# Two slots of 16 pairs in place of three, spare products on TensorE, and a first slot in three parts

## The reference

```python
# x, u: 8192 x 64, adj: 8192 x 8192, all float32
keep = (u >= 0.1)
x_drop = x * keep / 0.9
y = x + adj @ x_drop
out = (y - mean(y)) / sqrt(var(y) + 1e-5)      # over the 64 columns of each row
```

## Time and profile before

| | |
|---|---|
| median of 3 runs | 642.97 us |
| the profiled execution's own time | 643.25 us |
| its span, first to last instruction | 641.5 us |
| mean granted TensorE clock | 0.927 of full |
| TensorE busy | 514.2 us (80%) |
| VectorE, ScalarE, GpSimd busy | 48.6, 10.8, 18.0 us |
| DMA: moved, mean rate | 274.80 MB, 428 GB/s |

### The profile page before, as it was taken

How to read it: one execution, slowest core, us unless ns; L and a number is a source line. 1 busy time by engine, 2 the same in 40 slices (tenths; PEclk the granted TensorE clock), 3 DMA queues, 4 the chain that set the end, 5 groups by cost and what they waited for, 6 DMA issues and landing times.

```text
span 641.5 us, 5637 instructions
## 1 busy us (share of the span) xinstructions
PE 514.2 (80%) x2308; PEld 175.9 (27%) x2308; DVE 48.6 (8%) x230; ACT 10.8 (2%) x18; POOL 18.0 (3%) x27
## 2 busy tenths in 40 slices
PE   0397888778988797797788779788797788689796
PEld 0132223222222232232232223222232232223225
DVE  2100101010010100101010010100001010000102
ACT  0000000000000000000000000000000000000000
POOL 0000000000000000000000000000000000000000
PEclk9998888998979798898989989798898989989999
DMA  9999999999999999999999999999999999999998
GB/s 374 423 448 436 429 432 440 416 440 425 430 436 450 412 449 440 429 426 443 413 440 429 430 432 454 426 432 443 423 430 439 420 437 447 428 416 428 434 422 335
DMA packets 9962, 274.80 MB, mean 428 GB/s; under 512 B 1388, under 2 KB 1642, under 8 KB 2666
## 3 DMA queue, kind: packets, MB, share of 16 engines
q1 hardware_dynamic: 9660, 274.60, 99.5%
q10 hardware_dynamic: 300, 0.16, 0.1%
HBM read 272.66 MB, written 2.10 MB: 428 GB/s over the span
## 4 chain that ended last, share of the span: by engine, by line
DMA 70%; PE 27%; issue 1%; SPq 0%; DVE 0%; POOL 0%; POOLq 0%; ACT 0%; DVEq 0%
DMA raw<-adj_dram 70%; PE acc L173 26%; SPq L132 0%; PE turned L193 0%; POOL rstd L268 0%; DVE stats L238 0%; POOLq L47 0%; ACT sums L211 0%; DVE rows L234 0%; SPq L137 0%; SPq L135 0%; SPq L136 0%; DVE moments L243 0%; POOLq L273 0%; DVE final_normed L261 0%
## 5 line engine op out<-in xcount | busy, mean ns | idle before, releaser
L173 PE MATMUL acc<-raw,dropped 128*64 128x504 f32 x2048 | 488.5, 637 | 93.3 <-POOLq L273 89.3
L173 PEld LDWEIGHTS acc<-raw,dropped 128*64 128x64 f32 x2048 | 152.9, 147 | 417.2 <-issue 291.5
L234 DVE TENSOR_TENSOR rows<-turned,x_sb 126x256 f32<-126x256 f32 x16 | 6.8, 425 | 541.8 <-PE turned L193 541.8
L268 POOL TENSOR_TENSOR rstd<-var_eps,minus_half 126x4 f32<-126x4 f32 x16 | 16.2, 1013 | 613.4 <-DMA raw<-adj_dram 330.2
L193 PE MATMUL turned<-join,sums 128*126 128x64 f32 x128 | 17.5, 279 | 10.9 <-ACT sums L211 10.9
L193 PEld LDWEIGHTS turned<-join,sums 128*126 128x126 f32 x128 | 15.3, 189 | 24.8 <-ACT sums L211 24.8
L211 ACT COPY sums<-acc 128x504 f32<-128x504 f32 x16 | 9.3, 579 | 616.3 <-PE acc L173 616.3
L249 DVE TENSOR_SCALAR normed<-rows,moments,rstd 126x64 f32 x64 | 15.7, 310 | 29.4 <-POOL rstd L268 29.4
L183 PE MATMUL final_turned<-x_final,eye 128*128 128x64 f32 x2 | 0.7, 449 | 18.1 <-DVE dropped L229 18.1
L238 DVE BATCH_NORM_STATS2 stats<-rows 126x6 f32<-126x64 f32 x64 | 9.7, 214 | 0.5
L173 PE MATMUL final_acc<-raw,dropped 128*64 128x128 f32 x128 | 7.3, 274 | 0.0
(11 more groups left out here) (14 smaller groups left out, 2.6 us busy)
## 6 DMA issues: line engine op xcount, KB each, us to landing
raw<-adj_dram SPq DMA_DIRECT2D x30, 5544.0 KB, 26.8
raw<-adj_dram SPq DMA_DIRECT2D x14, 5040.0 KB, 29.0
raw<-adj_dram SPq DMA_DIRECT2D x2, 3024.0 KB, 21.9
raw<-adj_dram SPq DMA_DIRECT2D x2, 2520.0 KB, 27.5
raw<-adj_dram SPq DMA_DIRECT2D x2, 2016.0 KB, 23.6
raw<-adj_dram SPq DMA_DIRECT2D x2, 1512.0 KB, 26.9
dropped<-u_dram SPq DMA_DIRECT2D x1, 2048.0 KB, 7.8
x_sb<-x_dram SPq DMA_DIRECT2D x1, 2048.0 KB, 12.3
```

Of the source, the lines that this page charges most:

```text
L173: last = nc.tensor.matmul(sum_bank[t * D:(t + 1) * D, 0:width], dropped[:, t * PAIRS + q, :], raw[:, s, start:start + width], start=(q == ...
L234: nc.vector.tensor_tensor(rows[:, :, :], turned[0:ROWS, 0:GROUPS, :], x_sb[0:ROWS, bass.ds(b * GROUPS, GROUPS), :], ALU.add).then_inc(turn ...
L268: nc.gpsimd.tensor_tensor(rstd[:, :], var_eps[:, :], minus_half[0:ROWS, :], ALU.pow).then_inc(rstd_ready, 1)
```

## The change

raw has two slots of 16 pairs, 64,512 bytes (63 KB) a partition each, in place of three of 11, 11 and 10. Block 0's slot 0 is loaded in three parts of 6, 5 and 5 pairs, slot 1 whole; Pool passes the three parts ahead of its loop, and its later waits on slot 0's semaphore count one load less. In the last blocks slot 0 is loaded in three parts and slot 1 in five.

TensorE gets `keep_busy(times)`: products of 128 columns of weights with 504 columns, both read from dropped, into a bank of their own that nobody reads. It is called in every block: 5 products after slot 0, 1 after slot 1 (while ScalarE copies), and 3 after the turning products.

```diff
-SLOT_PAIRS = [(0, 11), (11, 22), (22, 32)]
+SLOT_PAIRS = [(0, 16), (16, 32)]
-PARTS = [(0, 0, 6), (0, 6, 11), (1, 11, 17), (1, 17, 22), (2, 22, 26), (2, 26, 29), (2, 29, 31), (2, 31, 32)]
+PARTS = [(0, 0, 6), (0, 6, 11), (0, 11, 16), (1, 16, 22), (1, 22, 26), (1, 26, 29), (1, 29, 31), (1, 31, 32)]
+IDLE_SLOT, IDLE_COPY, IDLE_TURNED = 5, 1, 3
+        spare = psum("spare", [P, 512])
@@ SP
-            for s in range(SLOTS):
-                load_slot(0, s)
+            for n, (s, q0, q1) in enumerate(PARTS):
+                if s == 0:
+                    load_part(0, n)
+            load_slot(0, 1)
@@ TensorE
+            def keep_busy(times):
+                for _ in range(times):
+                    nc.tensor.matmul(spare[:, 0:WIDTH], dropped[:, 0:TILES, :],
+                                     dropped[:, :, :].rearrange("p c d -> p (c d)")[:, 0:WIDTH],
+                                     start=True, stop=True)
                     if q1 == SLOT_PAIRS[s][1]:
                         last.then_inc(multiplied, 1)
+                        keep_busy(IDLE_SLOT if s == 0 else IDLE_COPY)
                 last.then_inc(block_turned, 1)
+                keep_busy(IDLE_TURNED)
@@ Pool
             def pass_slot(b, s):
-                pool.wait_ge(raw_loaded[s], b * DMA + DMA)
+                pool.wait_ge(raw_loaded[s], b * DMA if s == 0 else b * DMA + DMA)
                 pool.sem_inc(landed, IN_SLOT[s])
-            pass_slot(0, 0)
+            for n, (s, q0, q1) in enumerate(PARTS):
+                if s == 0:
+                    pass_part(n, 1)
             for n, (s, q0, q1) in enumerate(PARTS):
-                pass_part(n, 2 if s == SLOTS - 1 else 1)
+                pass_part(n, 2)
```

## The result

| | before | changed |
|---|---|---|
| median | 642.94 us (4 runs, 642.6 to 643.09) | 653.12 us (4 runs, 652.77 to 653.43) |
| the profiled execution's own time | 643.25 us | 652.93 us |
| its span | 641.5 us | 651.1 us |
| mean granted TensorE clock | 0.927 | 0.99 |

The changed kernel takes 1.0158 times as long (95% interval 1.0145 to 1.0170), 10.2 us by the medians. The forecast was 653.5.

A forecast was written before the change was run, and what follows sets the result against it. The stream of loads of raw sets the pace, not TensorE. Nothing changes in mid-kernel; 78.74 us of TensorE work at the end finishes 10.5 us later, so 642.97 + 10.5 = 653.5 us, range 646.5 to 658.7.

The forecast's parts named there:

- The end: Last two blocks: TensorE never waits after slot 0 of block 14 lands; final multiply ends at 646.5, 10.5 us later.
- The price of a spare product: Each keep_busy product on TensorE: 0.84 to 0.85 us, with bounds of 0.43 and 1.22 us.
- the sum: TensorE's work from block 14's first slot through the final multiply: slots, spare products, copies, turnings, multiply, 78.74 us together.
- The chain behind the last multiply: After the final multiply: copy, product, statistics and store stay at 5.5 us.
- The middle: Mid-kernel blocks: spare products cost nothing, since slots of 17.74 and 17.99 us fit 19.07 us of stream; clock at full.
- The equality of 40 and 44 KB rows: Loads of raw: both row lengths take 1.192 us a pair, so longer rows gain 0 to 0.9 us, set at zero.
- Two slots: Reloads of raw: issued 13.9 us after landing, plus 3.0 us latency, against 19.07 us: in time by 2.2 us.
- the starving of the stream: Rival for the reloads: 2.2 us more delay starves the stream; 1 us beyond gives 681 us; chance 4%.
- The start: Block 0: slot 1 starts cold at 53.0, ends at 69.7 instead of 66.7; 0 to 0.9 us lost once.
- The dear spare product: Rival for every block: a spare product costs 1.22 us, TensorE becomes the bound, 672 us; chance 5%.

The follow-up runs named there:

- the run with the warm start: Changed kernel with 16 spare products after slot 0 of block 0 instead of 5, and at the end only those idle time covers: 643.25 us, ratio 1.0009.
- The run with half rows: Kernel before with every whole slot loaded by two DMAs, rows of 20 and 24 KB instead of 40 and 44: 646.34 us, ratio 1.0051.

## Why the prediction came out right, point by point

**The end** was the step that mattered, and it held. Forecast: slot 0 of block 14 at 567.80, then 78.74 us without a wait to 646.5. Measured: 567.09, then 79.66 us to 646.75. The run without spare products in the last two blocks shows that this is the cause and the only one of size. Its terms, forecast and measured (from the fence of the end):

| | forecast | measured |
|---|---|---|
| 4 slots | 54.08 | 2 x 13.67 + 2 x 13.68 = 54.70 |
| spare products outside the copies | 13.52 | 2 x 4.42 + 2.68 + 2.69 = 14.21 |
| 2 copies | 1.80 | 0.94 + 0.95 = 1.89 |
| 2 turnings | 2.06 | 0.83 + 0.82 = 1.65 |
| final multiply | 7.28 | 7.21 |

The price of a spare product, 0.845 us, was right: sixteen in a row took 13.79 us in the run with the warm start and five took 4.49, so eleven more cost 9.30, 0.845 each. What the sum lacked stands where products of 64 and of 128 columns follow each other: 13.67 - 13.52 = 0.15 us behind a slot, and 4.42 - 5 x 0.845 = 0.20 behind a group of five. Where one slot follows another directly, it is 13.52 again (27.26 - 13.74, from the run without spare products in the last two blocks).

**The chain behind the last multiply** was taken as unchanged, 5.5 us. It was 651.1 - 646.75 = 4.35, 1.1 us less, for the reason that the run without the bulk store shows. Slot 0 of block 14 came 0.71 us earlier than forecast. That nearly cancels the underpriced terms (0.9 us), so the final multiply ended within 0.3 us of the forecast, 10.72 us later than before. The shorter chain is not cancelled: 10.72 - 1.12 = 9.6 us in the spans, 9.7 between the profiled executions, where I had 10.5 for both. The medians are 10.2 apart, because the profiled execution was 0.3 us above the median before the change and 0.2 below it after. That the median came to within 0.4 us of the forecast is in part luck; five more executions had a median of 653.96.

**The middle.** No cost of the spare products and a clock at full: both right. The equality of 40 and 44 KB rows misled me about the price of a row. The run with half rows shows 9 to 10 ns, yet the longer rows brought only 38.13 - 38.10 = 0.03 us a block (0.5 us in all) where 8 rows at that price would be 0.08. That lies inside the 0 to 0.9 us of the range; the sum had it at zero.

**Two slots.** I gave the starving of the stream 4%, with a margin of 2.2 us a slot. With spare products that held in mid-kernel. But the run without them shows how much hangs on the clock: I expected 643 us there and got 657. Two steps failed there. One is that half clock costs 1.7 us a slot: many bursts lost that, but others lost up to 2.9 (16.6 us in place of 13.74). The other is that 3.0 us ahead of the landing is in time for a reload: 3.6 to 3.9 us ahead, the stream still lost 1.3 to 1.9 in the stretch shown and behind it. So the margin of 2.2 us was an overestimate. The expectation for four products ahead of the release missed that a late landing cools TensorE.

**The start.** The forecast of a burst cold by 3.0 us (to 69.7) and 0 to 0.9 us lost: the burst took 15.31 us in one execution, cold by 1.6, and 16.69 in the other, cold by 3.0; the second was 1.65 us behind the first by block 14. Over the three slots from 51.8 us on, the first lost 0.9 us against 3 x 19.05 and the second 2.5, of which about 1 may be the late landing named below as left open. So the 0 to 0.9 us of that step was too narrow.

**One figure of a rival.** The dear spare product was to decide from 1.07 us on. From the sum's own terms a block is 2 x 13.52 + 1.03 + 9 x the price (the copy then lies under one of the nine), which reaches 38.14 at 1.12. Since the price measured 0.845, nothing hangs on it.

**Left open.** In the starts shown one landing near 52 or 72 us comes about 1 us late: 71.78 - 51.80 = 19.98 in the changed kernel, 52.95 instead of 51.8 with the warm start. So it does in the kernel before: from 26.80 to 52.99 are 26.19 us for 21 pairs, where 21 x 1.192 is 25.0. What holds it up isn't known. And the versions with two slots that spare the end have times spread over 2.1 to 3.3 us, where the kernel before stays within 1.4 beside them; the start accounts for 1.65 us between two executions of the changed kernel and for 1.25 between two that spare the end, but a warm start didn't remove the spread. No profile of one of the late executions with a warm start exists.

## What to carry to other kernels

Work that fills idle time in a loop is free only while something later than it is waited for. Cost it in the last iterations by themselves: there count from the last landing that the engine waits for, and add up everything behind it. When a ring of buffers is cut to two, the reload is due before the other buffer has landed by more than the latency of a load (here 3.0 us of latency, no loss at 5.1 us, losses at 3.3 to 3.9), and the work time that enters this sum is that of a cold engine unless something keeps it warm.

## What the runs showed of the hardware

- TensorE after short waits: with waits of 0.9 us ahead of bursts of 13.74 us the granted clock was 1.00 from 110 to 640 us in the changed kernel; with waits of 2.3 to 3.9 us it averaged 0.82 from 327.5 to 370 us in the run without spare products, and bursts took 16.6 us (row below). A single wait of that size needn't do it: behind one of 2.27 us the burst at 382.63 in the run with 2 products ahead of the release took 13.74 us.

```profile
327.50:370.00 42.50, 35.74 (x140) 11.66 (x142) 2.57 (x14) 0.58 (x1) 1.01 (x1) 0.82 1.00 411
```

- A warm TensorE alone buys nothing where the stream is the bound: with three slots and the clock at 1.0 in place of 0.927 the burst at 574.96 us came at 574.81.
- A float32 product of 128 columns by 504 takes 0.845 us (9.30 us for eleven), as long as a pair of products of 64 columns (0.845, from 17.97 us for 21 pairs and 9.52 for 11). The Trainium skill (TensorE: Matmul & The Clock Gate, Part 3: Packing small matmuls) says that small matmuls in different parts of the array run at the same time; the spare products, which take as long as such a pair, agree.
- A load of 16 pairs (8.26 MB) issued when nothing else was queued (the run with 4 products ahead of the release) landed after 22.06 us, 3.0 us more than the 19.05 that its bytes take in the running stream.
- A store of 32 KB lands 1.5 us after its issue on idle DMA engines and 2.5 us after it beside a running store with rows of 15 KB.
